# Four GpSimd instructions in halves, with new orders, PSUM homes and waits, in an attention and slot-mixture kernel

## The chip, the cores and the metric

One core of one Trainium2 chip. The metric is the device time of one execution in microseconds; the kernel before took 595.33 us (median of 3 runs, 594.32 to 596.03).

## The reference, cut to what matters

```python
x = x + layernorm(attention(layernorm(x)))          # x: 32 batches x 256 tokens x 128
x = x + layernorm(slot_mixture(layernorm(x)))

def attention(x):                                   # 16 heads of 8
    q, k, v = exp(x Wq' + bq), exp(x Wk' + bk), x Wv' + bv
    kv  = cumsum(k[:, :, :, None] * v[:, :, None, :], axis=1)   # outer products, summed over tokens
    k1  = cumsum(k, axis=1)
    out = einsum('zsD,zsDd->zsd', q, kv) / sum(q * k1)
    return out Wo' + bo

def slot_mixture(x):                                # 8 experts x 64 slots = 512 slots
    logits   = rms_norm(x) . rms_norm(slot_embeds)
    slots    = xn weighted by softmax(logits over tokens)       # "dispatch"
    hidden   = gelu(slots @ w1)                     # 512 wide
    out      = (hidden @ w2) weighted by softmax(logits over slots)  # "combine"
```

## The kernel before, in words

The kernel is written in raw instructions, one list for each engine, with a semaphore for nearly every kind of result. The unit of work is a batch of 256 tokens: partition p holds the tokens 2p and 2p+1 (the even and the odd token of a pair). There are 32 batches, and each goes through the stages below. Many batches are under way at once: in step `s` TensorE projects batch s, sums the keys of batch s-1, closes the attention of s-2, starts the slots of s-3, and does the hidden layer of s-4.

**The path of one batch n.**
- `x_statistics` (VectorE), `x_rstd_of` (GpSimd: a floor `x_ve` and a power `x_rs`), `x_normalise` (VectorE, writes `xh`), `x_transpose` (TensorE), `xT_high` (ScalarE) and `xT_low` (VectorE): the value is split into a high part and the rest, since a product is made of three matmuls (`three`, L800 to 804) to keep precision. Then `project(n, 0)` and `project(n, 1)`, and `qk_evict`, `v_evict` (ScalarE) into `E`.
- `shift_odd` (SyncE's DMA) moves the keys and values of the odd tokens one partition on, into `prev`.
- GpSimd builds the pair sums: `outer_odd` writes `kv_prev` from `prev`, `outer_even` writes `kv` from `E` (both through the helper `outer`, L211, 1024 elements a partition), `pair_sum` adds them (L380), `pair_keys` adds the keys (L374). ScalarE's `sums_high` copies them to `kv_hi` (L435), and GpSimd's `sums_low` writes the rest `kv_lo` (L318, 1152 elements). The two outer products, the pair sum and `sums_low` are GpSimd's four long instructions.
- `cumulate(n, k)` for k = 2, 0, 1 (TensorE, a triangular matrix) makes the running sums in PSUM (`CU[k]`), `multiply(n, k)` (VectorE) multiplies each with q into `prod`, `attention_sums` reduces `prod` into `ND` in PSUM. `own_product` (GpSimd), `own_sum` (VectorE), `own_value` (GpSimd) make the even token's share of its own pair; `attention` adds it and divides.
- `att_transpose`, `attT_copy`, `attention_out`, `y_squares`, `y_rstd_of` (GpSimd), `first_residual` (VectorE), `x1_squares`, `x1_rstd_of` (GpSimd: a floor, then a power), `x1_normalise` (VectorE, writes `xn`), `xn_transpose`, `xnT_high`, `xnT_low`, `logits`.
- `slot_maxima` and `part_maxima` (VectorE), `dispatch_exp` (ScalarE), `part_transpose`, `token_maxima`, `subtract_max`, `dispatch_scale` (VectorE: a reciprocal, and a multiply of `disp_t` by it, L1331), `dispatch_transpose`, `dispatch_copy`, `combine_exp`, `gather_slots`, `slT_high`, `slT_low`, `hidden(n, f)` for four f, `gelu(n, f)`, `process`, `proc_copy`, `mixture`, `o_squares`, `o_rstd_of`, `second_residual`, `store`.

**What sets the order.** Each engine has its own list: `first_steps`, then `step(s)` for all s, then `last_steps` (some engines have none). An engine does its list strictly in order. A stage waits only where its producer isn't known to be done by another wait already made; that is why many waits stand under `if n in (...)`. ScalarE changes its table between the exponentials and the GELUs twice a step (`gelu_table`, `exp_table`, L426 and L430).

**PSUM.** Eight banks are named by hand (L147 to L161). Tensors that share a bank can't be alive together; before, the running sums 1 and 2 share bank 5, so that `cumulate(n, 1)` waits until `multiply(n, 2)` has read the bank.

`spin(k)` runs k matmuls on the identity whose result nobody reads. They fill TensorE's idle time in `first_steps`.

Of the kernel before, what the change touches and what calls it, by code (L numbers as in the profile page):

```python
# [5 lines left out]
def attention_and_slot_mixture(  # L6
# [7 lines left out]
    F32 = mybir.dt.float32  # L14
# [37 lines left out]
    with ctx:  # L52
# [6 lines left out]
        def sem(name):  # L59
# [99 lines left out]
        HP = [banks[:, 6, :], banks[:, 0, :], banks[:, 6, :], banks[:, 4, :]]  # L159
        PR = banks[:, 6, :].rearrange("p (j d) -> p j d", d=DIM)  # L160
        OB = banks[:, 5, 0:NC * YW].rearrange("p (c d) -> p c d", d=YW)  # L161
# [22 lines left out]
        xT_lo_ready, qk_exp, v_copied, kv_even, kv_odd, kv_den = (  # L184
            sem("s_" + n) for n in ("xTlo", "qkexp", "vcopy", "kve", "kvo", "kvd"))
        kv_built, kv_hi_ready, kv_lo_ready, qk_own_ready, own_den, own_ready = (
            sem("s_" + n) for n in ("kv", "kvhi", "kvlo", "qkown", "ownden", "own"))
        own_added, summed, den_ready, att_ready, att_T, attT_ready = (
            sem("s_" + n) for n in ("ownadd", "summed", "deninv", "att", "attTp", "attT"))
        wo_done, y_var, y_rstd, x1_ready, x1_var, x1_floor = (  # L190
            sem("s_" + n) for n in ("wo", "yve", "yrs", "x1", "x1ve", "x1fl"))
        x1_rstd, xn_ready, xnT_done, xnT_hi_ready, xnT_lo_ready, lb_done = (
            sem("s_" + n) for n in ("x1rs", "xn", "xnT", "xnThi", "xnTlo", "lb"))
        max_ready, part_ready, partT_done, tok_ready, lb_shifted, disp_exp = (
            sem("s_" + n) for n in ("max", "part", "partT", "tok", "lbs", "dexp"))
        disp_inverted, disp_scaled, slT_done, slT_hi_ready, slT_lo_ready, proc_ready = (
            sem("s_" + n) for n in ("dinv", "dscale", "slT", "slThi", "slTlo", "procs"))
        mix_done, o_var, o_rstd, res_ready, x_stat = (
            sem("s_" + n) for n in ("mix", "ove", "ors", "res", "xstat"))
# [28 lines left out]
        def _(sp):  # L228
# [45 lines left out]
        def _(pool):  # L274
# [1194 lines left out]
```

## Time and profile before

| what | value |
|---|---|
| median of three runs | 595.33 us |
| the profiled execution: own time, span | 594.64 us, 592.9 us |
| TensorE busy, share of the span | 557.5 us, 94% |
| VectorE | 484.2 us, 82% |
| ScalarE | 473.4 us, 80% |
| GpSimd | 473.1 us, 80% |
| instructions | 10573 |

In the profile PE is TensorE's matmuls and PEld its weight loads, DVE is VectorE, ACT ScalarE, POOL GpSimd, SP SyncE. A line number is one of the kernel before. Where an arrow stands between two tiles, the left one is written from the right one. The 1.7 us between span and own time are outside the first and last instruction.

### The profile page before, as it was taken

The numbers are of one execution on the slowest core, as the hardware profiler recorded it, in microseconds if no ns is written. First come the engines' busy times: TensorE is split into PE (matmuls) and PEld (weight loads), VectorE is DVE, ScalarE is ACT, GpSimd is POOL, SyncE is SP. The second block draws the span as 40 slices with busy tenths as digits, with TensorE's granted clock in tenths as the row PEclk, the third lists the DMA queues.
The fourth block names the chain that finished last, engine by engine and source line by source line (L and its number), as shares of the span: only waits on it lengthen the run. The fifth ranks groups of instructions, "written<-read, shape, count | busy, mean of one in ns | idle before, by whom it ended". The sixth has DMA issues, their size and how long they took to land.

```text
span 592.9 us, 10573 instructions
## 1 busy us (share of the span) xinstructions
PE 557.5 (94%) x3772; PEld 486.1 (82%) x3772; DVE 484.2 (82%) x922; ACT 473.4 (80%) x1244; POOL 473.1 (80%) x462
## 2 busy tenths in 40 slices
PE   7937999999999999999999999999999999999886
PEld 7925898888888898888888988888888988887775
DVE  4897888888988888888888888889888888878430
ACT  3255889988888889888888899888888888888663
POOL 4777888889888988889888888898888888974100
PEclk9958999999999999999999999999999999999999
DMA  4000000000000000000000000000000000000000
GB/s 115 10 19 19 19 9 19 19 28 28 27 28 28 10 28 18 28 28 28 28 27 28 10 26 20 28 28 28 28 27 12 26 19 28 19 26 10 11 9 19
DMA packets 16825, 14.29 MB, mean 24 GB/s; under 512 B 2850, under 2 KB 16644, under 8 KB 16772
## 3 DMA queue, kind: packets, MB, share of 16 engines
q1 hardware_dynamic: 14708, 12.76, 7.1%
q10 hardware_dynamic: 2064, 0.86, 0.6%
q8 instruction: 30, 0.49, 0.3%
q14 instruction: 23, 0.19, 0.1%
HBM read 5.25 MB, written 4.19 MB: 16 GB/s over the span
## 4 chain that ended last, share of the span: by engine, by line
PE 42%; POOL 23%; ACT 19%; DVE 10%; issue 3%; DMA 1%; SPq 0%; POOLq 0%; DVEq 0%; ACTq 0%
POOL kv_lo L318 11%; PE banks L929 9%; PE banks L955 8%; POOL x_rs L296 7%; ACT kv_hi L422 6%; ACT L430 6%; PE banks L802 5%; PE banks L804 5%; PE banks L803 5%; DVE prod L1253 4%; ACT hid L447 3%; DVE xh L1157 3%; PE banks L782 3%; PE banks L881 2%; ACT disp_t L545 2%
## 5 line engine op out<-in xcount | busy, mean ns | idle before, releaser
L942 PE MATMUL banks<-w_c,hid 128*128 128x128 f32 x1024 | 124.6, 276 | 2.4 <-ACT hid L447 2.4
L942 PEld LDWEIGHTS banks<-w_c,hid 128*128 128x128 f32 x1024 | 119.2, 192 | 3.5 <-ACT hid L447 2.2
L318 POOL TENSOR_TENSOR kv_lo<-kv,kv_hi 128x1152 fp32r<-128x1152 f32 x31 | 81.7, 2636 | 32.5 <-ACT kv_hi L422 32.5
L1253 DVE TENSOR_TENSOR prod<-banks,E 128x768 f32<-128x768 f32 x96 | 88.3, 948 | 1.9 <-PE banks L882 1.9
L1268 DVE TENSOR_REDUCE banks<-prod 128x288 f32<-128x2304 f32 x32 | 81.5, 2545 | 0.0
L212 POOL TENSOR_TENSOR kv_prev<-prev 128x1024 f32<-128x1024 f32 x31 | 66.8, 2153 | 10.5 <-DMA prev<-E 10.5
L955 PEld LDWEIGHTS banks<-proc,comb 128*128 128x128 f32 x512 | 61.1, 191 | 17.0 <-DVE prod L1253 14.9
L380 POOL TENSOR_TENSOR kv<-kv,kv_prev 128x1024 f32<-128x1024 f32 x31 | 74.7, 2410 | 0.0
L447 ACT ACTIVATE hid<-banks 128x512 f32<-128x512 f32 x128 | 70.5, 612 | 4.8 <-PE banks L804 2.0
L212 POOL TENSOR_TENSOR kv<-E 128x1024 f32<-128x1024 f32 x32 | 68.6, 2144 | 4.1 <-ACT E L422 2.2
L1318 DVE TENSOR_REDUCE neg_max<-banks 128x4 f32<-128x1024 f32 x32 | 39.2, 1224 | 31.2 <-PE banks L804 31.2
L955 PE MATMUL banks<-proc,comb 128*128 128x129 f32 x512 | 62.5, 275 | 0.8 <-ACT proc L422 0.8
L929 PE MATMUL banks<-disp,xn 128*128 128x512 f32 x128 | 60.7, 597 | 1.1 <-ACT disp L422 1.0
L545 ACT ACTIVATE disp_t<-banks,neg_max 128x256 f32<-128x256 f32 x128 | 58.9, 474 | 0.0
L802 PE MATMUL banks<-slT_hi,w_hi 128*128 128x512 f32 x128 | 54.7, 427 | 0.2 <-DVE slT_lo L1178 0.2
L422 ACT ACTIVATE disp<-banks 128x512 f32<-128x512 f32 x64 | 34.7, 595 | 23.4 <-PE banks L910 23.4
L881 PE MATMUL banks<-kv_hi,tri 128*128 128x384 f32 x96 | 41.4, 432 | 10.7 <-DVE prod L1253 9.3
L804 PE MATMUL banks<-slT_hi,w_lo 128*128 128x512 f32 x128 | 50.7, 396 | 0.0
L803 PE MATMUL banks<-slT_lo,w_hi 128*128 128x512 f32 x128 | 50.6, 395 | 0.0
L296 POOL TENSOR_TENSOR x_rs<-x_ve,minus_half 128x2 f32<-128x2 f32 x32 | 47.9, 1495 | 2.7
L346 POOL TENSOR_TENSOR o_rs<-o_ve,minus_half 128x2 f32<-128x2 f32 x32 | 22.8, 712 | 29.1 <-ACT o_sq L482 29.1
L426 ACT ACT_TABLE_LOAD x31 | 39.8, 1283 | 0.6
(140 smaller groups left out, 1516.9 us busy)
## 6 DMA issues: line engine op xcount, KB each, us to landing
X<-in_L_attn_x_dram SPq DMA_DIRECT2D x32, 128.0 KB, 2.1
out_dram<-res SPq DMA_DIRECT2D x32, 128.0 KB, 2.0
prev<-E SPq DMA_DIRECT2D x32, 112.0 KB, 2.1
w_in<-in_L_ffn_w_dram ACTq DMA_DIRECT2D x2, 256.0 KB, 4.6
prev<-E SPq DMA_DIRECT2D x32, 15.0 KB, 2.0
se_in<-n_L_ffn_slot_embeds_dram ACTq DMA_DIRECT2D x1, 256.0 KB, 3.2
w_in<-in_L_attn_Wq_dram SPq DMA_DIRECT2D x1, 64.0 KB, 2.4
w_in<-in_L_attn_Wk_dram SPq DMA_DIRECT2D x1, 64.0 KB, 2.2
```

The costliest lines, as they stand in the source:

```text
L212: return eng.tensor_tensor(dst.rearrange("p (d h e) -> p d h e", d=HD, h=NH), k.rearrange("p (o h e) -> p o h e", o=1, h=NH).broadcast_to( ...
L296: pool.tensor_tensor(x_rs[:, :], x_ve[:, :], minus_half[:, 0:NC], ALU.pow).then_inc(x_rstd, 1)
L318: pool.tensor_tensor(kv_lo[:, :], kv[:, :], kv_hi[:, :].bitcast(F32), ALU.subtract)\
L447: act.activation(hid[:, f, :], HP[f], ACT.Gelu).then_inc(gelu_ready[f], 1)
L802: pe.matmul(dst, a_hi, b_hi, start=start, stop=False, skip_group_check=True)
L803: pe.matmul(dst, a_hi, b_lo, start=False, stop=False, skip_group_check=True)
L804: return pe.matmul(dst, a_lo, b_hi, start=False, stop=stop, skip_group_check=True)
L929: last = pe.matmul(SL, xn[n % 2][:, c, :], disp[:, c, :], start=(c == 0), stop=(c == NC - 1))
L942: last = pe.matmul(PR[:, j, :], hid[:, f, j * P:(j + 1) * P], w2_c[:, f, :], start=(f == 0), stop=(f == FJ - 1))
L955: last = pe.matmul(OB[:, c, :], comb[n % 2][:, j, c * P:(c + 1) * P], proc[:, j, 0:YW], start=(j == 0), stop=(j == SJ - 1))
L1253: dve.tensor_tensor(prod[u][:, :, d0 * DIM:d1 * DIM].rearrange("p c (d f) -> p c d f", d=g), CU[k].rearrange("p (o d f) -> p o d f", o=1, ...
L1268: dve.tensor_reduce(ND.rearrange("p c f h -> p c (f h)"), prod[n % 2][:, :, :].rearrange("p c (f e) -> p c f e", e=HD), AX.X, ALU.add).the ...
```

## The change

Four kinds of edit, made together.

1. **Halves.** `outer` gets a parameter `parts`; GpSimd's two outer products, its pair sum and its `sums_low` are two instructions of half the length each, and the semaphore is raised by the second. The first batch's outer product on VectorE stays whole.
2. **Orders.** In GpSimd's step `x_rstd_of`, `o_rstd_of` come ahead of `sums_low`, and `own_product` and `y_rstd_of` behind it; `own_value` comes ahead of `outer_even`. In VectorE's step `x_normalise` comes ahead of `dispatch_scale`, `own_sum` behind `x1_normalise`, `attention` goes to the start of the next step ahead of the maxima, and the part maxima come ahead of the slot maxima. In TensorE's step `cumulate(., 1)` comes behind the next `x_transpose`, `hidden(., 3)` ahead of `hidden(., 0)`, and `att_transpose` between the two projections. In ScalarE's step `v_evict` comes directly behind `qk_evict`.
3. **PSUM homes.** The running sum 1 has bank 1 and no longer shares with sum 2; the outputs, transposes and hidden tiles move.
4. **Waits** follow the new orders: `cumulate(n, 1)` waits for `x1_ready` of n-1 (bank 1's last reader) in place of `prod_ready`; `dispatch_exp` waits for `max_ready`; `hidden(n, 3)` waits for `slT_lo_ready`; `project(n, 1)` waits for `gelu_ready[2]`.

The first steps get more `spin` (73 in place of 8 after the first running sum), and `last_steps` fall away on VectorE and ScalarE and are written anew on GpSimd.

```diff
-        XT = banks[:, 1, 0:SEQ]
-        XN = banks[:, 3, 0:SEQ]
-        PT = banks[:, 7, 0:SEQ]
-        CU = [banks[:, 6, 0:DU * DIM], banks[:, 5, 0:DU * DIM], banks[:, 5, 0:DU * DIM]]
+        XT = banks[:, 4, 0:SEQ]
+        XN = banks[:, 6, 0:SEQ]
+        PT = banks[:, 5, 0:SEQ]
+        CU = [banks[:, 6, 0:DU * DIM], banks[:, 1, 0:DU * DIM], banks[:, 5, 0:DU * DIM]]
...
-        HP = [banks[:, 6, :], banks[:, 0, :], banks[:, 6, :], banks[:, 4, :]]
+        HP = [banks[:, 4, :], banks[:, 0, :], banks[:, 1, :], banks[:, 1, :]]
...
+        def outer(eng, dst, k, v, parts=1):
+            w = HD // parts
+            for d in range(0, HD, w):
+                last = eng.tensor_tensor(
+                    dst[:, d * DIM:(d + w) * DIM].rearrange("p (d h e) -> p d h e", d=w, h=NH),
+                    k.rearrange("p (o h e) -> p o h e", o=1, h=NH).broadcast_to((P, w, NH, HD)),
+                    v.rearrange("p (h d o) -> p d h o", d=HD, o=1)[:, d:d + w].broadcast_to((P, w, NH, HD)), ALU.mult)
+            return last
...
             def sums_low(n):
                 pool.wait_ge(kv_hi_ready, n + 1)
-                pool.tensor_tensor(kv_lo[:, :], kv[:, :], kv_hi[:, :].bitcast(F32), ALU.subtract)\
+                for f in (slice(0, FEAT // 2), slice(FEAT // 2, FEAT)):
+                    last = pool.tensor_tensor(kv_lo[:, f], kv[:, f], kv_hi[:, f].bitcast(F32), ALU.subtract)
+                last\
                     .then_inc(kv_lo_ready, 1)
...
             def pair_sum(n):
                 pool.wait_ge(kv_even, n + 1)
-                pool.tensor_tensor(kv[:, 0:KVF], kv[:, 0:KVF], kv_prev[:, :], ALU.add).then_inc(kv_built, 1)
+                for f in (slice(0, KVF // 2), slice(KVF // 2, KVF)):
+                    last = pool.tensor_tensor(kv[:, f], kv[:, f], kv_prev[:, f], ALU.add)
+                last.then_inc(kv_built, 1)
...
             def step(s):                      # GpSimd
                 x_rstd_of(s)
+                o_rstd_of(s - 6)
+                sums_low(s - 2)
+                x_negative(s - 2)
+                own_product(s - 2)
                 y_rstd_of(s - 3)
                 outer_odd(s - 1)
                 x1_rstd_of(s - 3)
                 pair_keys(s - 1)
-                x_negative(s - 2)
+                own_value(s - 2)
                 outer_even(s - 1)
-                own_value(s - 2)
                 pair_sum(s - 1)
-                o_rstd_of(s - 5)
-                own_product(s - 1)
-                sums_low(s - 1)
...
             def step(s):                      # VectorE
                 x_statistics(s)
+                attention(s - 3)
+                part_maxima(s - 4)
+                slot_maxima(s - 4)
                 second_residual(s - 6)
                 token_maxima(s - 4)
-                own_sum(s - 2)
+                x_normalise(s)
                 dispatch_scale(s - 4)
-                x_normalise(s)
                 multiply(s - 2, 2)
                 first_residual(s - 3)
                 multiply(s - 2, 0)
                 multiply(s - 2, 1)
                 xT_low(s)
                 x1_normalise(s - 3)
+                own_sum(s - 2)
                 slT_low(s - 4)
                 attention_sums(s - 2)
                 xnT_low(s - 3)
-                attention(s - 2)
-                slot_maxima(s - 3)
-                part_maxima(s - 3)
...
             def step(s):                      # TensorE
                 x_transpose(s)
+                cumulate(s - 2, 1)
                 gather_slots(s - 4)
                 mixture(s - 5)
                 xn_transpose(s - 3)
+                hidden(s - 4, 3)
                 hidden(s - 4, 0)
-                hidden(s - 4, 3)
                 hidden(s - 4, 1)
                 hidden(s - 4, 2)
                 logits(s - 3)
                 project(s, 0)
+                att_transpose(s - 2)
                 project(s, 1)
-                att_transpose(s - 2)
...
                 cumulate(s - 1, 0)
-                cumulate(s - 1, 1)
...
             def step(s):                      # ScalarE
                 exp_table(s)
                 sums_high(s - 2)
                 qk_evict(s - 1)
+                v_evict(s - 1)
                 attT_copy(s - 3)
                 dispatch_exp(s - 4)
-                v_evict(s - 1)
...
                 xT_high(s)
+                combine_exp(s - 4, 1)
                 slT_high(s - 4)
-                combine_exp(s - 4, 1)
                 gelu_table(s - 4)
                 xnT_high(s - 3)
+                gelu(s - 4, 3)
                 o_squares(s - 5)
                 gelu(s - 4, 0)
-                gelu(s - 4, 3)
...
             def cumulate(n, k):
...
                 elif k == 1:
-                    pe.wait_ge(prod_ready[2], n + 1)
+                    if n == 0:
+                        after(pe, v_copied, n + 1)
+                    after(pe, x1_ready, n - 1)
...
             def dispatch_exp(n):
-                act.wait_ge(part_ready, n + 1)
-                if n == 30:
-                    act.wait_ge(max_ready, n + 1)
+                act.wait_ge(max_ready, n + 1)
```

## Rows read from the trace of the kernel before

**Rows 1.** The page: busy time and share of the span.

```profile
PE 557.5 (94%) x3772; PEld 486.1 (82%) x3772; DVE 484.2 (82%) x922; ACT 473.4 (80%) x1244; POOL 473.1 (80%) x462
```

**Rows 2.** Timeline, ScalarE: `sums_high` of batches 2 and 31 (start, duration).

```profile
48.12 1.16 ACT L422 ACTIVATE kv_hi<-kv 128x1152 fp32r<-128x1152 f32 x1
...
533.85 1.16 ACT L422 ACTIVATE kv_hi<-kv 128x1152 fp32r<-128x1152 f32 x1 [0.68 <-POOL kv L380]
```

**Rows 3.** The chain of waits in one step (start, length in us, what).

```profile
300.66 2.63 POOL kv_lo L318
...
303.65 1.66 POOL x_rs L296
...
305.33 0.60 DVE xh L1157 x2
```

**Rows 4.** Windows: stretch, length; busy (count) PE, PEld, DVE, ACT, POOL; clock, DMA, GB/s.

```profile
97.99:114.32 16.33, 16.33 (x115) 14.52 (x114) 14.62 (x29) 14.41 (x39) 14.61 (x15) 1.00 0.09 26
299.42:316.20 16.78, 16.49 (x115) 14.45 (x114) 14.65 (x29) 14.57 (x38) 15.00 (x15) 1.00 0.08 25
```

**Rows 5.** The waits, whole span: total, times, longest in us.

```profile
PEld banks L881 <- DVE prod L1253: 18.5, 29, 2.2
```

**Rows 6.** Timeline, VectorE and GpSimd where their instructions overlap.

```profile
303.51 1.23 DVE L1331 TENSOR_TENSOR disp_t<-disp_t,disp_inv 128x1024 f32<-128x1024 f32 x1
...
102.22 0.70 POOL L296 TENSOR_TENSOR x_rs<-x_ve,minus_half 128x2 f32<-128x2 f32 x1
102.89 1.16 POOL L334 TENSOR_TENSOR y_rs<-y_ve,minus_half 128x2 f32<-128x2 f32 x1
...
102.25 1.24 DVE L1331 TENSOR_TENSOR disp_t<-disp_t,disp_inv 128x1024 f32<-128x1024 f32 x1
...
19.90 2.55 POOL L212 TENSOR_TENSOR kv_prev<-prev 128x1024 f32<-128x1024 f32 x1 [0.79 <-DMA prev<-E]
...
20.38 2.15 DVE L1157 TENSOR_SCALAR xh<-X,x_mv,x_rs 128x128 f32<-128x128 f32 x1
...
309.48 0.46 POOL L374 TENSOR_TENSOR kv<-E,prev 128x128 f32<-128x128 f32 x1
309.55 0.48 DVE L1299 TENSOR_SCALAR xn<-x,x_mv,x_rs 128x128 f32<-128x128 f32 x1
```

**Rows 7.** Groups of GpSimd's instructions, 200 to 400 us: count, busy, mean ns, idle.

```profile
L318 POOL TENSOR_TENSOR kv_lo<-kv,kv_hi 128x1152 fp32r<-128x1152 f32 x12 | 31.6, 2637 | 12.3 <-ACT kv_hi L422 12.3
L380 POOL TENSOR_TENSOR kv<-kv,kv_prev 128x1024 f32<-128x1024 f32 x12 | 29.0, 2417 | 0.0
...
L326 POOL TENSOR_TENSOR own<-E,own 128x128 f32<-128x128 f32 x12 | 6.7, 558 | 0.0
```

**Rows 8.** Timeline of GpSimd, VectorE and TensorE in the step of rows 3.

```profile
306.26 2.15 POOL L212 TENSOR_TENSOR kv_prev<-prev 128x1024 f32<-128x1024 f32 x1 [0.29 <-DMA prev<-E]
...
308.80 0.71 POOL L341 TENSOR_TENSOR x_rs<-x_vf,minus_half 128x2 f32<-128x2 f32 x1
...
302.72 0.28 DVE L1262 TENSOR_REDUCE own<-qk_own 128x16 f32<-128x128 f32 x1
...
310.21 0.68 DVE L1178 TENSOR_TENSOR slT_lo<-banks,slT_hi 128x512 fp32r<-128x512 f32 x1
...
311.14 0.19 PEld L802 LDWEIGHTS banks<-slT_hi,w_hi 128*128 128x128 f32 x1
...
317.44 2.64 POOL L318 TENSOR_TENSOR kv_lo<-kv,kv_hi 128x1152 fp32r<-128x1152 f32 x1 [1.06 <-ACT kv_hi L422]
```

**Rows 9.** The first steps: a window's row, and the chain's row on the spins.

```profile
35.00:40.00 5.00, 3.28 (x12) 2.67 (x12) 4.13 (x11) 1.51 (x8) 3.93 (x5) 0.50 0.08 28
...
15.07 8.93 PE banks L782 x80
```

**Rows 10.** Timeline, the last batch: VectorE's slot maxima and ScalarE's table load.

```profile
566.76 1.22 DVE L1318 TENSOR_REDUCE neg_max<-banks 128x4 f32<-128x1024 f32 x1 [2.00 <-PE banks L804]
...
568.07 1.28 ACT L545 ACT_TABLE_LOAD   x1
```

More of the change, by code:

```diff
@@ L190, in attention_and_slot_mixture @@
[L190 to L197, printed above, removed]
@@ new lines, in attention_and_slot_mixture @@
+        y_var, y_rstd, x1_ready, x1_var, x1_floor, x1_rstd = (
+            sem("s_" + n) for n in ("yve", "yrs", "x1", "x1ve", "x1fl", "x1rs"))
+        xn_ready, xnT_done, xnT_hi_ready, xnT_lo_ready, lb_done, max_ready = (
+            sem("s_" + n) for n in ("xn", "xnT", "xnThi", "xnTlo", "lb", "max"))
+        part_ready, partT_done, tok_ready, lb_shifted, disp_exp, disp_inverted = (
+            sem("s_" + n) for n in ("part", "partT", "tok", "lbs", "dexp", "dinv"))
+        disp_scaled, slT_done, slT_hi_ready, slT_lo_ready, proc_ready, mix_done = (
+            sem("s_" + n) for n in ("dscale", "slT", "slThi", "slTlo", "procs", "mix"))
@@ L201, in after @@
+        o_var, o_rstd, res_ready, x_stat = (
+            sem("s_" + n) for n in ("ove", "ors", "res", "xstat"))
         def after(eng, s, n):
@@ L406, in step, with last_steps @@
                 pair_keys(s - 1)
-                x_negative(s - 2)
+                own_value(s - 2)
                 outer_even(s - 1)
-                own_value(s - 2)
                 pair_sum(s - 1)
-                o_rstd_of(s - 5)
-                own_product(s - 1)
-                sums_low(s - 1)
+            def last_steps():
+                x_rstd_of(31)
+                o_rstd_of(25)
+                sums_low(29)
+                x_negative(29)
+                own_product(29)
+                y_rstd_of(28)
+                outer_odd(30)
+                pair_keys(30)
+                x1_rstd_of(28)
+                own_value(29)
+                outer_even(30)
+                pair_sum(30)
+                o_rstd_of(26)
+                sums_low(30)
+                x_negative(30)
+                own_product(30)
+                y_rstd_of(29)
+                outer_odd(31)
+                x1_rstd_of(29)
+                pair_keys(31)
+                own_value(30)
+                outer_even(31)
+                pair_sum(31)
+                o_rstd_of(27)
+                sums_low(31)
+                x_negative(31)
+                own_product(31)
+                y_rstd_of(30)
+                x1_rstd_of(30)
+                own_value(31)
+                o_rstd_of(28)
+                y_rstd_of(31)
+                x1_rstd_of(31)
+                o_rstd_of(29)
+                o_rstd_of(30)
+                o_rstd_of(31)
             first_steps()
-            for s in range(3, 37):
+            for s in range(5, 31):
                 step(s)
+            last_steps()
         @block.scalar
@@ L773, in _ @@
             first_steps()
-            for s in range(8, 33):
+            for s in range(6, 37):
                 step(s)
-            last_steps()
         @block.tensor
@@ L1128, in _ @@
             first_steps()
-            for s in range(6, 32):
+            for s in range(6, 34):
                 step(s)
```

421 lines of the change are left out of this document (125 added, 296 removed).

## The prediction

> **What bounds the kernel now.** I read the page's busy times first [rows 1]: TensorE leads with 94%, but three others lie at 80 to 82%, and an average doesn't say which wait ends last. So next the pace of the steps. ScalarE's `sums_high` stands at 48.12 us for batch 2 and at 533.85 for batch 31 [rows 2]: 485.73 us for 29 steps, 16.75 each; 48 us lie ahead of it and 59 behind. Then the chain of waits inside one step [rows 3]. It doesn't stay on TensorE: it goes `kv_lo` 2.63 and `x_rs` 1.66 on GpSimd, `xh` 0.60 and `prod` on VectorE, and by the running sum 1, gather, mixture and hidden matmuls on TensorE back to ScalarE and `kv_hi`. That ring is one step long.
>
> The windows of two steps show what the ring costs [rows 4]. Both hold 115 matmuls. The usual one is 16.78 us long, the rare one 16.33, and in the rare one TensorE is busy for all of it: 16.33 is TensorE's own length of a step, the floor. The 0.45 between them is where `cumulate(n, 1)` waits for `multiply(n, 2)` to empty bank 5, 18.5 us in 29 waits over the span [rows 5].
>
> The timeline says why `x_rs` takes 1.66 [rows 6]. `disp_t` (VectorE, both inputs in SBUF) runs from 303.51 to 304.74; `x_rs` starts at 303.65 [rows 3] and ends at 305.31, 0.57 after it. In the rare step `x_rs` started 0.03 ahead of `disp_t` and took 0.70, and the next one, `y_rs`, took 1.16 and ended 0.56 after `disp_t`. So a small GpSimd instruction that comes second stands until `disp_t` is over. The other way round, `xh` started at 20.38 under a long GpSimd instruction (19.90 to 22.45) and took 2.15, to 22.53, 0.08 after it. Behind a short one (0.46, from 309.48) `xn` took 0.48 where one of a free pair takes some 0.34 (0.60 for two [rows 3]): 0.14 lost, so the short one gives way 0.21 after its start.
>
> **The change part by part.**
>
> *Bank 1 for sum 1, moved behind the next transpose.* The wait of rows 5 goes. `cumulate(n, 1)` now waits for `x1_ready` of n-1, a pair of 0.3 us instructions done before `multiply(n, 0)`, and has the transpose as slack. If this were all that binds, a step would take TensorE's 16.33: 29 x (16.75 - 16.33) = 12.2 us gained.
>
> *`x_rstd` ahead of `sums_low`.* It leaves the ring of rows 3 with 2.63 + 1.66: it is done while ScalarE still writes `kv_hi`, and `x_normalise` no longer waits for it. What is late next is the rest of GpSimd's list.
>
> *The halves.* What does one more instruction cost? The pair sum takes 2.42 for 1024 elements [rows 7], the pair keys 0.46 for 128 [rows 6]: 2.19 ns an element, 0.18 fixed. The outer product, 2.15 for 1024 [rows 8]: (2.15 - 0.46) / 896 = 1.89 ns, 0.22 fixed. Instructions in a row overlap by 0.03 [rows 6]. So a split adds 0.14 to the pair sum, 0.19 to each outer product, and 0.14 to `sums_low`, 0.66 a step. Nearest rows for bounds: 0 (the fixed part wholly hidden in the first half) and 0.46 each, a whole 128-element instruction. I take 0.66, since both shapes give it. The gain of halves is that a VectorE instruction held by GpSimd waits for half.
>
> *Who holds whom in the new order.* Let e be the end of `sums_low`. Take the step's first hidden matmul, 311.14, as zero: `sums_low` starts at 6.3 (317.44), and its first half ends at 7.7. `x_normalise` now comes behind `token_maxima`, where `own_sum` stood before: 302.72 + 16.78 = 319.50, at 8.4 [rows 8]. So `xh` arrives in the second half and stands until e: first of the pair done at e+0.08, second 0.26 later, reciprocal 0.2, and `disp_t` may start at e+0.47. GpSimd does `x_negative` and then starts `own_product` at about e+0.45 (an estimate from its 0.19 us, its 0.07 gaps and `xh` in between). It is first by a hair; as with `xn`, it gives way 0.21 after its start. `disp_t` runs e+0.68 to e+1.91. `y_rstd` waits for it: e+2.47 (the 0.56 above). Then the ring through GpSimd goes on:
> - `outer_odd` 2.15 + 0.19 less the overlap: e+4.77 [rows 8]. Its DMA is early, since `v_evict` moved ahead of the exponentials.
> - `x1_rstd`: 306.26 + 2.15 = 308.41 to 308.80 + 0.71 = 309.51 [rows 8], 1.10: e+5.87.
> - `xn` pair behind the pair keys, 309.55 to 310.21 [rows 6, 8], 0.66, and 0.04 to wake: e+6.57. `own_sum` 0.28 [rows 8] and 0.05: e+6.90. `own_value`, now ahead of `outer_even`, waits for it (the pair keys cover 0.46 of this 1.03): 0.56 [rows 7], e+7.42.
> - `outer_even` 2.15 + 0.19: e+9.76. `pair_sum` is directly behind, so its wait costs 0.07, then 2.42 + 0.14: e+12.39.
> - `x_rstd` free of `disp_t` 1.01, `o_rstd` 0.66: e+14.06. `sums_low` 2.64 + 0.14 less overlap 0.02: e+16.82.
>
> So the ring through GpSimd alone is 16.82 us, 0.49 above TensorE's floor. A second ring goes by `slT_low`: 0.68 from e+6.85 and 0.05, then 6.3 from the first hidden matmul to `sums_low` (311.14 to 317.44), and 2.76: 6.85 + 0.73 + 6.3 + 2.76 = 16.64 [rows 8]. It is shorter and hidden. The first one decides: 29 x (16.82 - 16.75) = +2.0 us. The released bank is worth nothing then: TensorE waits elsewhere, 0.49 a step ahead of the dispatch transposes and the hidden matmuls.
>
> *A rule weighed.* In the rows only a VectorE instruction with one SBUF tensor is held by GpSimd; `disp_t` never comes second. The Trainium skill, "SBUF — State Buffer", section "Who interferes with whom", says that a VectorE instruction with two SBUF inputs and a GpSimd one that reads SBUF exclude each other whichever is first. By it `own_product` holds `disp_t` as in the sum; without it `disp_t` ends 0.21 earlier and the ring is 16.61. Rows 6 agree with one direction (`x_rs` held 0.93), no row shows the other.
>
> *First steps.* Until 24 us all goes as before (39 spins in place of 40; a spin is 8.93 / 40 = 0.22 us [rows 9]). Behind it 73 spins come in place of 8, 14.5 us more, in idle time of TensorE of about that length. They keep the clock up: it was 0.50 between 35 and 40 us [rows 9]. `logits(0)` is on the chain at half speed and gets back some 1.4 us, but `w1_low`, `wo_centre` now stand ahead of `bo_centre` on VectorE, and `pair_sum(2)` ends some 1 us later. I take -0.5 (bounds -3, full clock and the halves' shorter stand; +3, spins that overrun a wait).
>
> *The end.* For batch 31 ScalarE's exponentials waited for the slot maxima, done at 567.98, while the table load started at 568.07 behind a GELU [rows 10]. Now the part maxima come first, 1.14 (566.76 to 567.90, where they stood second): +1.1 on the path to the end. Bounds 0 and +3 for the rest of the redone tail.
>
> *Edits at nothing.* `hidden(., 3)` first, `att_transpose` between the projections and `combine_exp` ahead of `slT_high` move equal work along queues with slack of 0.2 or more; if that is gone, TensorE waits up to 0.2 a step, still under its 0.49 of spare time. `attention` in the next step fills VectorE's wait for the logits (about 1 us). `v_evict` ahead of `attT_copy` puts 0.3 before a transpose that has it.
>
> Sum: 594.64 + 2.0 - 0.5 + 1.1 = 597.2 us against the profiled execution; that one lies 0.7 under the median of the three runs, so 597.5 is as good. I say 597.3.
>
> **The rivals.**
>
> *TensorE takes over (faster).* If halves in a row hide their fixed part (0.66 off: 16.16), or `xh` slips in between the halves of `sums_low` so that `disp_t` starts by e, the GpSimd ring falls under 16.33 and TensorE decides. 29 x 0.42 = 12.2 off: 594.64 - 12.2 + 0.6 = 583; with half of the split cost hidden, 16.49, 588. For it: TensorE's 16.33 has been seen [rows 4]. Against it: both fixed costs read the same from two shapes.
>
> *`disp_t` first, `own_product` held (slower).* The race at e+0.45 against e+0.47 can go the other way. Then `disp_t` ends at e+1.70, `own_product` 0.32 behind it and `y_rs` 0.70 later, at e+2.74 in place of 2.47. The ring is 17.09: 29 x 0.34 = 9.9 over, 605. It decides from the point where `x_negative` loses 0.02 more. For it: `x_rs` lost just such a race in nearly every step.
>
> *VectorE's pair of SBUF inputs isn't held by GpSimd.* Ring 16.61, 29 x 0.14 = 4.1 off, 591.
>
> **How the numbers follow.** Chances: the forecast 0.45, its own range 592 to 601 by 0.15 a step either way; TensorE's floor 0.25; `disp_t` first 0.20; not held 0.10. Within 0.3% is 593.5 to 597.1, about what can be told from no change. The forecast lies at its upper edge, so of its 0.45 I give 0.10 to faster, 0.15 to the same, 0.20 to slower. Faster: 0.10 + 0.25 + 0.08 = 0.43. Same: 0.15 + 0.02 = 0.17. Slower: 0.20 + 0.20 = 0.40. The range 584 to 604.5 leaves out the lowest of TensorE's case and the upper edge of the race.
>
> **What would show it.** The wait of `cumulate(., 1)` on `prod` is gone. `x_rs` takes 0.70 and `y_rs` more than 1, ending 0.56 behind `disp_t`. One of the `xh` pair takes over 0.7. Halves of about 1.18 and 1.3. GpSimd is over 90% busy with next to no idle before `kv_lo`, steps of 16.8. Steps of 16.3 with TensorE always busy, or `own_product` at 1.4 us, would prove a rival. It is wrong at its root if neither engine shows longer instructions where the two overlap.

## The result, and the profile after

The changed kernel takes 592.36 us against 595.2 for the one before, each the median of 20 executions side by side: a ratio of 0.9948, 95% interval 0.9933 to 0.9963. It is 0.5% faster. The prediction was 597.3 us, 0.3% slower: the range held the time, and the sign was wrong. The interval lies clear of no change.

The page after: busy times, and the shares of the chain that ended last.

```profile
PE 567.5 (96%) x3908; PEld 501.8 (85%) x3908; DVE 509.7 (86%) x922; ACT 470.7 (80%) x1244; POOL 493.5 (84%) x587
...
POOL 74%; DVE 8%; PE 7%; issue 5%; ACT 4%; DMA 1%; SPq 0%; POOLq 0%; DVEq 0%
```

TensorE still leads in the first line, as in [rows 1], but the chain lies on GpSimd for 74% of the span. That TensorE is the busiest engine says nothing here of which one sets the pace. Next `kv_hi` of batches 2 and 31 (timeline, ScalarE), to set beside [rows 2].

```profile
47.69 1.16 ACT L484 ACTIVATE kv_hi<-kv 128x1152 fp32r<-128x1152 f32 x1 [2.27 <-POOL kv L382]
...
532.56 1.16 ACT L484 ACTIVATE kv_hi<-kv 128x1152 fp32r<-128x1152 f32 x1 [1.05 <-POOL kv L382]
```

With the spans (592.9 before, 590.2 after) these rows cut the difference in three, the cuts of the prediction's own sum:

| stretch | before | after | difference | predicted |
|---|---|---|---|---|
| to `kv_hi` of batch 2 | 48.12 | 47.69 | -0.43 | -0.5 |
| 29 steps | 485.73 | 484.87 | -0.86 | +2.0 |
| behind `kv_hi` of batch 31 | 59.05 | 57.64 | -1.41 | +1.1 |

The chain of waits through one step after (start, length, what; against [rows 3]), from the start of one `kv_lo` to the next:

```profile
299.45 2.75 POOL kv_lo L319 x2
...
302.54 0.45 POOL qk_own L352
303.00 1.64 POOL y_rs L335
304.63 2.26 POOL kv_prev L213 x2
...
308.03 0.73 DVE xn L1216 x2
...
309.04 0.52 POOL own L327
309.56 2.26 POOL kv L213 x2
...
311.88 2.54 POOL kv L382 x2
...
314.78 0.71 POOL x_rs L296
315.49 0.67 POOL o_rs L347
316.16 1.39 POOL kv_lo L319
```

It is the ring that the prediction drew, piece by piece: all of it on GpSimd, but for `xn` and `own_sum`, and 16.71 long from 299.45 to 316.16. In this step it never goes to TensorE. (A length in the chain leaves out what overlaps with the piece before; the timeline's lengths of the same instructions are up to 0.04 longer.) What holds `y_rs` at 1.64 is seen in the timeline of VectorE and GpSimd (e, the end of `sums_low`, is 302.20):

```profile
301.12 1.44 DVE L1075 TENSOR_SCALAR xh<-X,x_mv,x_rs 128x128 f32<-128x128 f32 x2
...
302.54 0.45 POOL L352 TENSOR_TENSOR qk_own<-E 128x128 f32<-128x128 f32 x1
302.67 1.40 DVE L1246 TENSOR_TENSOR disp_t<-disp_t,disp_inv 128x1024 f32<-128x1024 f32 x1
302.95 1.68 POOL L335 TENSOR_TENSOR y_rs<-y_ve,minus_half 128x2 f32<-128x2 f32 x1
```

`xh` takes 1.44 for the pair where it took 0.60 in [rows 3], and ends at 302.56, behind e. `disp_t` starts 0.13 behind `own_product` (tile `qk_own`) and takes 1.40 where it took 1.23 in [rows 6]. `y_rs` ends 0.56 behind `disp_t`.

TensorE's waits after, whole span. The row of [rows 5] has none that answers to it; this one stands in its place (0.44 a step on the weight loads):

```profile
PEld banks L863 <- DVE disp_t L1246: 13.6, 31, 0.9
```

### The profile page after: what moved, and what is told of

Read it like the earlier page. It is cut to its first block, busy times and chain, and to the rows that moved or that the text cites. A ratio compares the mean times of both kernels' runs of the same rounds, so it can differ in the third digit from the quotient of the medians.

```text
span 590.2 us, 10874 instructions
## 1 busy us (share of the span) xinstructions
PE 567.5 (96%) x3908; PEld 501.8 (85%) x3908; DVE 509.7 (86%) x922; ACT 470.7 (80%) x1244; POOL 493.5 (84%) x587
## 4 chain that ended last, share of the span: by engine, by line
POOL 74%; DVE 8%; PE 7%; issue 5%; ACT 4%; DMA 1%; SPq 0%; POOLq 0%; DVEq 0%
POOL kv_lo L319 13%; POOL kv L382 12%; POOL kv_prev L213 11%; POOL kv L213 11%; POOL y_rs L335 8%; DVE xn L1216 4%; POOL x_rs L342 4%; POOL x_rs L296 3%; POOL o_rs L347 3%; POOL own L327 3%; POOL qk_own L352 2%; PE banks L743 2%; POOL x_vf L340 1%; DVE own L1179 1%; ACT disp_t L602 1%
## 5 line engine op out<-in xcount | busy, mean ns | idle before, releaser
L319 POOL TENSOR_TENSOR kv_lo<-kv,kv_hi 128x576 fp32r<-128x576 f32 x62 | 86.0, 1409 | 2.1 <-ACT kv_hi L484 2.1
L511 ACT ACTIVATE hid<-banks 128x512 f32<-128x512 f32 x128 | 73.5, 606 | 13.1 <-PE banks L764 12.7
L382 POOL TENSOR_TENSOR kv<-kv,kv_prev 128x512 f32<-128x512 f32 x62 | 78.8, 1292 | 2.4
L213 POOL TENSOR_TENSOR kv<-E 128x512 f32<-128x512 f32 x64 | 73.3, 1167 | 2.1 <-ACT E L484 2.1
L213 POOL TENSOR_TENSOR kv_prev<-prev 128x512 f32<-128x512 f32 x62 | 70.8, 1160 | 0.2 <-DMA prev<-E 0.2
L883 PE MATMUL banks<-disp,xn 128*128 128x512 f32 x128 | 63.0, 614 | 1.5 <-ACT disp L484 1.5
L335 POOL TENSOR_TENSOR y_rs<-y_ve,minus_half 128x2 f32<-128x2 f32 x32 | 52.0, 1624 | 10.8 <-ACT y_sq L529 10.8
L1228 DVE TENSOR_REDUCE part_max<-banks 128x256 f32<-128x1024 f32 x32 | 39.2, 1225 | 9.0 <-PE banks L764 6.4
L1246 DVE TENSOR_TENSOR disp_t<-disp_t,disp_inv 128x1024 f32<-128x1024 f32 x32 | 44.3, 1384 | 1.1
L1075 DVE TENSOR_SCALAR xh<-X,x_mv,x_rs 128x128 f32<-128x128 f32 x64 | 41.6, 690 | 1.1 <-POOL x_rs L296 1.1
```

The lines of the kernel that those rows point to most:

```text
L213: last = eng.tensor_tensor(dst[:, d * DIM:(d + w) * DIM].rearrange("p (d h e) -> p d h e", d=w, h=NH), k.rearrange("p (o h e) -> p o h e", ...
L319: last = pool.tensor_tensor(kv_lo[:, f], kv[:, f], kv_hi[:, f].bitcast(F32), ALU.subtract)
L335: pool.tensor_tensor(y_rs[:, :], y_ve[:, :], minus_half[:, 0:NC], ALU.pow).then_inc(y_rstd, 1)
L382: last = pool.tensor_tensor(kv[:, f], kv[:, f], kv_prev[:, f], ALU.add)
L511: act.activation(hid[:, f, :], HP[f], ACT.Gelu).then_inc(gelu_ready[f], 1)
L883: last = pe.matmul(SL, xn[n % 2][:, c, :], disp[:, c, :], start=(c == 0), stop=(c == NC - 1))
```

## The experiments

Names: "after" is the changed kernel. Every time is the median of a kernel's executions, and every ratio is against the kernel before, executed on the same chip in the same round of runs; its medians there were 595.3 to 595.7.

### 1. What each group of edits is worth alone

**All four long instructions whole again**, the rest as after (`a_whole`):

```diff
-                for f in (slice(0, FEAT // 2), slice(FEAT // 2, FEAT)):     # sums_low
+                for f in (slice(0, FEAT),):
-                outer(pool, kv[:, 0:KVF], ..., 2)                           # outer_even, outer_odd too
+                outer(pool, kv[:, 0:KVF], ...)
-                for f in (slice(0, KVF // 2), slice(KVF // 2, KVF)):        # pair_sum
+                for f in (slice(0, KVF),):
```

> The changed kernel with its four long GpSimd instructions whole again, all else kept. Theory 1 (the ring through GpSimd is 16.70 us a step and a split costs 0.11 or 0.12 on it, four times): the ring falls by 0.45 to 16.25, TensorE's 16.33 takes over, steps of 16.33 to 16.40, total 9 to 11 us less than the changed kernel (about 582), idle time before kv_lo comes back. Theory 2 (the halves are what gained, since VectorE stands for half as long): xh and disp_t stand longer, steps of 16.8 or more, total 3 us or more above the changed kernel.

Measured: 581.95 us, ratio 0.9776 (0.9753 to 0.9798). A window of 200 us (busy times of PE, PEld, DVE, ACT, POOL; after, PE has 197.51 there), and behind it one `kv_lo` in the timeline:

```profile
200.00:400.00 200.00, 200.00 (x1379) 177.68 (x1378) 187.84 (x342) 176.44 (x464) 183.50 (x171) 1.00 0.09 25
```

```profile
294.33 2.64 POOL L319 TENSOR_TENSOR kv_lo<-kv,kv_hi 128x1152 fp32r<-128x1152 f32 x1 [0.20 <-ACT kv_hi L484]
```

TensorE is busy for all of it, steps are 16.38, and GpSimd waits 0.20 for `kv_hi` in each. The halves cost 10.4 us here. The other edits together are worth 13.3 (595.2 to 581.95). How they share it between orders, PSUM homes and spins is not shown by these two kernels.

**The other way round: the kernel before with the four halves and nothing else** (`b_halves`; the same edits as in the change's diff).

> The kernel before with the four instructions in halves and nothing else. Theory 1: its ring holds one split, that of sums_low, 0.11 a step; the other three (0.35) fit in the 1.05 us idle before kv_lo. Steps of 16.89, total 3.2 us more than before (1.005). Theory 2 (halves gain by themselves): the same or less than before.

Measured: 604.11 us, ratio 1.0144 (1.0122 to 1.0166), steps of 17.06. Slower as expected, but by 8.6 in place of 3.2. Timeline, GpSimd and the `disp_t` of the same step:

```profile
306.10 2.78 POOL L322 TENSOR_TENSOR kv_lo<-kv,kv_hi 128x576 fp32r<-128x576 f32 x2 [0.84 <-ACT kv_hi L428]
308.97 1.26 POOL L297 TENSOR_SCALAR x_ve<-x_mv 128x2 f32<-128x2 f32 x1
310.31 0.70 POOL L299 TENSOR_TENSOR x_rs<-x_ve,minus_half 128x2 f32<-128x2 f32 x1
...
308.95 1.22 DVE L1337 TENSOR_TENSOR disp_t<-disp_t,disp_inv 128x1024 f32<-128x1024 f32 x1
```

The split of `sums_low` pushed `x_ve` 0.02 behind the start of `disp_t`, so both `x_ve` and, after it, `x_rs` come late: from the end of `kv_lo` to the end of `x_rs` it is 2.13 here and 2.02 in the kernel before ([rows 3]: 303.29 to 305.31). With the split itself (2.78 for 2.64) that makes 0.25 of the 0.28 a step.

### 2. What a split costs, and where

Two kernels with some halves only. **Only `sums_low` in halves** (`a_half_low`), and **only the two outer products** (`a_half_outer`):

```diff
 # a_half_low: outer_even, outer_odd, pair_sum as in a_whole; sums_low keeps
                 for f in (slice(0, FEAT // 2), slice(FEAT // 2, FEAT)):
 # a_half_outer: sums_low, pair_sum as in a_whole; both outer products keep
                 outer(pool, ..., 2)
```

> The kernel after with three of the four long GpSimd instructions whole again; only sums_low stays in two halves. Theory 1 (a split adds 0.11 to 0.12 us to GpSimd's list, and the step is the longer of GpSimd's ring and TensorE's 16.38): with all four whole GpSimd has 0.20 us of idle time ahead of kv_lo in a step of 16.38, so its list is 16.18; one split makes it 16.29, still under 16.38. Steps of 16.38, idle time ahead of kv_lo about 0.09, total 582, the same as with all four whole. Theory 2 (every split costs its share, a quarter of the 10.4 us between the kernel after and the one with four whole): 16.46 a step, 584.6.

> The kernel after with sums_low and the pair sum whole again; only the two outer products stay in halves. Theory 1: GpSimd's list is 16.18 + 2 x 0.115 = 16.41, 0.03 over TensorE's 16.38: steps of 16.41 to 16.45, total 583 to 584, no idle time of GpSimd ahead of kv_lo, each outer product 2.26 in two. Theory 2 (every split costs a quarter of the 10.4 us): 16.54 a step, 587.

Measured: 586.64 us (ratio 0.9842, 0.9816 to 0.9868) with steps of 16.52, and 584.47 us (0.9808, 0.9783 to 0.9832) with steps of 16.44. The second has theory 1's steps, and lies 0.5 above its time. The first fell outside both theories. Its rows, a wait of TensorE over the span and one `kv_lo`:

```profile
PEld banks L863 <- DVE disp_t L1246: 9.4, 31, 0.9
```

```profile
296.62 2.77 POOL L319 TENSOR_TENSOR kv_lo<-kv,kv_hi 128x576 fp32r<-128x576 f32 x2 [0.19 <-ACT kv_hi L484]
```

GpSimd still idles 0.19 ahead of `kv_lo`, so its list isn't the bound, and yet a step is 0.14 longer. The weight loads of the dispatch transposes (L863) wait for `disp_t` in 31 batches; in `a_whole` the same row has only 4. So there is a second ring (not the prediction's, which went by `slT_low`): through `sums_low`, `xh`, `disp_t`, the dispatch transposes and the TensorE work behind them to `kv_hi`. `sums_low` lies in both rings, the other three only in GpSimd's. The split of `sums_low` costs its full 0.14 a step; the two of the outer products cost 0.06 together, since in `a_whole` GpSimd's list had 0.2 of idle time for them.

What a split costs must be read like for like. The timeline's lengths of the four pairs of halves, after:

```profile
299.42 2.78 POOL L319 TENSOR_TENSOR kv_lo<-kv,kv_hi 128x576 fp32r<-128x576 f32 x2
...
304.60 2.29 POOL L213 TENSOR_TENSOR kv_prev<-prev 128x512 f32<-128x512 f32 x2
...
309.51 2.29 POOL L213 TENSOR_TENSOR kv<-E 128x512 f32<-128x512 f32 x2
311.88 2.54 POOL L382 TENSOR_TENSOR kv<-kv,kv_prev 128x512 f32<-128x512 f32 x2
```

The same of `a_whole`, beside its `kv_lo` of 2.64 above:

```profile
290.00 2.40 POOL L382 TENSOR_TENSOR kv<-kv,kv_prev 128x1024 f32<-128x1024 f32 x1
...
299.37 2.14 POOL L213 TENSOR_TENSOR kv_prev<-prev 128x1024 f32<-128x1024 f32 x1
...
304.13 2.15 POOL L213 TENSOR_TENSOR kv<-E 128x1024 f32<-128x1024 f32 x1
```

`sums_low` 0.14 more, the outer products 0.15 and 0.14, the pair sum 0.14: a split costs GpSimd 0.14, whichever of the four it is, 0.56 a step for all. The steps say the same. GpSimd's list in `a_whole` is 16.38 less 0.20 of idle time and the 0.03 that it would overlap without it, 16.15; with two splits it is 16.44 (`a_half_outer`), with four 16.71. The 0.11 and 0.12 of the expectations came from setting the chain's lengths of the halves (2.75, 2.26) against the timeline's of the whole ones.

### 3. The new bank

**`cumulate(n, 1)` waits for `multiply(n, 2)` again**, in after (`a_prodwait`) and in `a_whole` (`a_whole_prodwait`), where TensorE is the bound and a late bank would show:

```diff
                     after(pe, x1_ready, n - 1)
+                    pe.wait_ge(prod_ready[2], n + 1)
```

> The changed kernel in which cumulate(n, 1) waits again for multiply(n, 2), as if it still shared its bank; its place behind the transpose is kept. Theory 1 (the bank's release is worth nothing as long as GpSimd's ring is longer than TensorE's step): TensorE waits 0.1 to 0.5 a step for prod, and the total stays within 0.5 us of the changed kernel, at 592. Theory 2 (the release is what gained): 5 to 12 us more.

> The kernel after with all four long instructions whole, where cumulate(n, 1) also waits for multiply(n, 2), as it had to while it shared a bank with the running sum 2. Here TensorE is the bound (busy for the whole of a step), so a late bank would be seen. Theory 1: multiply(n, 2) ends at 316.09 and cumulate(n, 1) starts after the transposes at some 316.8, 0.7 later: the wait is over when it comes, steps stay at 16.38, total 582 within 0.5; the new bank is worth nothing, and the old wait of 0.6 came from a late xh ahead of multiply(n, 2). Theory 2 (the new bank is what lets TensorE run without a gap): steps of 16.6 or more, 588 and above.

Measured: 592.98 us (0.9951, 0.9931 to 0.9971) against after's 592.36, and 582.62 us (0.9773, 0.9749 to 0.9798) against 581.95, with steps of 16.71 and 16.38. The 0.62 and 0.67 more are a little over the 0.5 allowed, but in the profiled executions the first running sum, ahead of the edit's first place, is already 0.67 and 0.60 later (24.02 to 24.69, 24.11 to 24.71), so that isn't the edit's. The 0.1 to 0.5 a step that TensorE was to wait for `prod` didn't come: in both kernels it waits for it once, 0.6 us in the first steps. In its new place the wait costs nothing that can be measured. What let TensorE off the 18.5 us of [rows 5] are the orders. The edit puts back the wait alone: sum 1 keeps bank 1, and `cumulate(n, 1)` its wait for `x1_ready`, which came with it. What the bank would have been worth in the old place wasn't tried.

### 4. The orders

**`own_product` ahead of `sums_low`**, in after (`a_own_first`) and in `a_whole` (`a_whole_own_first`):

```diff
+                own_product(s - 2)
                 sums_low(s - 2)
                 x_negative(s - 2)
-                own_product(s - 2)
```

> The changed kernel with own_product moved ahead of sums_low in GpSimd's step, halves kept. Theory 1 (what stands between the end of sums_low and outer_odd is priced by who holds whom): nothing holds disp_t (1.23 in place of 1.40), y_rs starts ahead of it and takes 0.70 in place of 1.68, the first half of outer_odd stands until disp_t is over. The ring loses about 0.9 there and gets 0.45 in front of sums_low: 16.25 to 16.35, total 9 to 11 us less than the changed kernel. Theory 2 (only GpSimd's sum of work counts, an order is worth nothing): steps of 16.7 and no difference.

> The kernel after with all four long instructions whole and own_product ahead of sums_low. GpSimd's 0.20 of idle time ahead of sums_low takes 0.20 of own_product's 0.45, so sums_low starts 0.25 later in both rings; disp_t is not held (1.23 in place of 1.41), y_rs takes 0.70. Theory 1 (TensorE's ring by sums_low and disp_t decides): 16.38 + 0.25 - 0.18 = 16.45 a step, 584. Theory 2 (GpSimd's list decides, and it gets shorter by 1.0): TensorE's 16.38 stays the bound, 582.

Measured: 592.64 us (0.9955, 0.9936 to 0.9973), where 9 to 11 less were expected, and 582.35 us (0.9775, 0.9750 to 0.9799), theory 2's. Timeline of `a_own_first`:

```profile
300.59 0.46 POOL L352 TENSOR_TENSOR qk_own<-E 128x128 f32<-128x128 f32 x1
301.00 2.78 POOL L319 TENSOR_TENSOR kv_lo<-kv,kv_hi 128x576 fp32r<-128x576 f32 x2
...
302.51 1.63 DVE L1075 TENSOR_SCALAR xh<-X,x_mv,x_rs 128x128 f32<-128x128 f32 x2
...
304.12 0.70 POOL L335 TENSOR_TENSOR y_rs<-y_ve,minus_half 128x2 f32<-128x2 f32 x1
304.25 1.22 DVE L1246 TENSOR_TENSOR disp_t<-disp_t,disp_inv 128x1024 f32<-128x1024 f32 x1
...
306.22 1.09 ACT L484 ACTIVATE disp<-banks 128x512 f32<-128x512 f32 x2 [1.10 <-PE banks L863]
...
308.15 0.23 POOL L340 TENSOR_SCALAR x_vf<-x_v 128x2 f32<-128x2 f32 x1 [0.53 <-ACT x_sq L537]
```

`disp_t` and `y_rs` came as expected in `a_own_first`, 1.22 and 0.70, and the time didn't move. With e = 303.78, the end of `sums_low`, `x_vf` starts at e+4.37, where it was e+4.77 after: of the 0.9 only 0.40 is gained, since GpSimd now waits 0.53 for ScalarE's `x_sq`. That stands behind the dispatch copies (tile `disp`) in ScalarE's list, these wait for the dispatch transposes, and these for `disp_t` (TensorE waits for it 14.8 us in 30 waits); `xh` ahead of `disp_t` is held to e. And `own_product` puts 0.41 ahead of `sums_low`, from 300.59 to 301.00. 0.40 less and 0.41 more: the step is 16.73. This isn't the second ring of `a_half_low`, since GpSimd doesn't wait for `kv_hi` here: it is GpSimd's own list from `x_vf` to e, closed by `xh`, `disp_t`, the transposes, the copies and `x_sq`. So the number is theory 2's, the reason isn't.

In `a_whole_own_first` `disp_t` takes 1.22, but `y_rs`, late by a wait of 0.29 for ScalarE, starts 0.10 behind it and takes 1.68, not 0.70. TensorE's 16.38 is the bound with or without this edit.

**`x_rstd` back behind `sums_low`**, in `a_whole` (`a_whole_xr_back`):

```diff
-                x_rstd_of(s)
                 o_rstd_of(s - 6)
                 sums_low(s - 2)
+                x_rstd_of(s)
```

> The kernel after with all four long instructions whole and x_rstd back behind sums_low, as before the change. Theory 1 (in the new order xh is made between sums_low and disp_t, and TensorE's ring runs by sums_low, xh, disp_t and the dispatch transposes; it is 16.38 long with disp_t starting 0.47 behind the end e of sums_low): x_rs now ends at e + 1.0, the xh pair takes 0.6, disp_t starts at e + 1.85, 1.4 later; its own stand of 0.18 goes. Steps of 17.6 to 17.8, total 612 to 622, with TensorE waiting for disp_t over 1 us a step. Theory 2 (GpSimd has the same work in either order, and only its sum counts): 16.4 a step, 582.

Measured: 619.38 us, ratio 1.0401 (1.0375 to 1.0428), steps of 17.78, and 43.4 us of the wait for `disp_t`: theory 1. Given the rest of the new order, this one move is worth 37.4 us. It can't be read as its worth in the kernel before, which had `disp_t` ahead of `xh`.

**`disp_t` ahead of `xh`**, as before, in `a_whole` (`a_whole_disp_first`):

```diff
-                x_normalise(s)
                 dispatch_scale(s - 4)
+                x_normalise(s)
```

> The kernel after with all four long instructions whole and disp_t's multiply ahead of xh on VectorE, as before the change. token_maxima ends at 296.31 in the step where sums_low runs from 294.33 to 296.97, so disp_t starts at about 296.5, second, under a long GpSimd instruction. Theory 1 (GpSimd's instruction holds it): disp_t takes 1.23 + 0.47 = 1.7 us, to 298.2; x_negative stands behind it, own_product comes at 298.7 and y_rs ends near 299.9 in place of 299.40: GpSimd's list 16.18 + 0.5 = 16.7 a step, total near 590. Theory 2 (disp_t is not held by a GpSimd instruction that came first): disp_t takes 1.23, ends at 297.7, and the total is 582 to 585.

Measured: 593.18 us, ratio 0.9959 (0.9944 to 0.9975), steps of 16.79, the pace of the kernel before. The size lay near theory 1's, its mechanism didn't occur:

```profile
302.96 0.18 DVE L1244 RECIPROCAL disp_inv<-disp_sum 128x4 f32<-128x4 f32 x1 [0.83 <-ACT disp_t L602]
303.12 0.46 POOL L352 TENSOR_TENSOR qk_own<-E 128x128 f32<-128x128 f32 x1
303.18 1.49 DVE L1246 TENSOR_TENSOR disp_t<-disp_t,disp_inv 128x1024 f32<-128x1024 f32 x1
...
305.97 0.59 DVE L1208 SCALAR_TENSOR_TENSOR x<-banks,y_rs,X 128x128 f32<-128x128 f32 x2
```

```profile
PEld banks L839 <- DVE x L1208: 13.7, 31, 0.5
```

`disp_t` waited for ScalarE's exponentials until `sums_low` was over (302.79), and `xh`, `multiply(n, 2)` and `first_residual` (tile `x`) stood behind it. The second fence is TensorE's wait in this kernel, in every step: the running sum 1 (L839) waits for `first_residual`, the last reader of its new bank 1. So here the wait that came with the new PSUM home does bind. In `a_whole` `xh` fills VectorE's wait for the exponentials, and `first_residual` comes in time (0.6 us in 3 waits). Whether a long GpSimd instruction holds `disp_t` for its whole length stays open; the two rows with the short one give 1.40 and 1.49.

The other moves of the change (`hidden(., 3)`, `att_transpose`, `own_value`, `v_evict`, `attention`) weren't tried one by one.

### 5. The two ends

**8 spins in place of 73** behind the first running sum, in `a_whole` (`a_whole_few_spins`):

```diff
-                spin(27)
+                spin(3)
...
-                spin(7)      # and 1, 4, 7, 12, 12, 3 left out
+                spin(5)
```

> The kernel after with all four long instructions whole and, behind the first running sum, 8 spin matmuls as before the change in place of 73. Theory 1 (the spins keep TensorE's clock up in the first steps): the granted clock between 30 and 45 us is 0.50 to 0.67 in place of 1.00, and kv_hi of batch 2 starts 1 to 2 us later than 47.3; the total 583 to 584. Theory 2 (the first steps are bound by VectorE and GpSimd, and TensorE's clock does not show in the time): clock down as well, kv_hi of batch 2 within 0.3 of 47.3, total 582.

Measured: 583.70 us (0.9796, 0.9771 to 0.9822) against 581.95. The clock fell, to 0.73 over 30 to 45 us where 0.50 to 0.67 was expected, from 1.00 in `a_whole` (TensorE was busy 6.59 us of the 15 there, in place of 14.55). `kv_hi` of batch 3, in `a_whole` and then with few spins:

```profile
63.76 1.17 ACT L484 ACTIVATE kv_hi<-kv 128x1152 fp32r<-128x1152 f32 x1
```

```profile
65.91 1.17 ACT L484 ACTIVATE kv_hi<-kv 128x1152 fp32r<-128x1152 f32 x1
```

It is 2.15 later. 0.85 of that is there already at `kv_hi` of batch 1 (29.51 and 30.36), and the first running sum, ahead of any spin left out, is as late (24.11 and 25.00). So it isn't the spins' doing: that mark lies anywhere from 29.15 to 30.65 in the kernels here. The other 1.30 come between batches 2 and 3, one batch later than expected, and up to batch 2 the pace is the same (17.80). There `logits(0)` takes 2.73 (45.86 to 48.59, clock 0.50 over 45 to 50 us) in place of 1.53 (44.96 to 46.49, clock 1.00). So the spins are worth 1.3 us by this one pair of profiled executions; the medians differ by 1.75.

**A single wait for batch 30** in the kernel before (`b_one_wait`):

```diff
-                act.wait_ge(part_ready, n + 1)
                 if n == 30:
                     act.wait_ge(max_ready, n + 1)
+                else:
+                    act.wait_ge(part_ready, n + 1)
```

> The kernel before, where the exponentials of batch 30 wait for the slot maxima alone in place of both maxima's semaphores; nothing else differs. Theory 1 (a table load goes ahead of a single wait, and stays behind the first of two): the table load of batch 30 starts behind the last GELU ahead of it, near 549 to 551 in place of 552.61, and the exponentials start 1.2 to 1.3 us earlier; about 1.2 us less in all, in the stretch behind kv_hi of batch 31. Theory 2 (the load's place has nothing to do with the waits): table load still at 552.6, no change.

Measured: 594.17 us (0.9967, 0.9950 to 0.9984). Timeline, the kernel before and then this one:

```profile
550.18 1.23 DVE L1312 TENSOR_REDUCE part_max<-banks 128x256 f32<-128x1024 f32 x1 [1.05 <-PE banks L804]
...
551.32 1.21 DVE L1318 TENSOR_REDUCE neg_max<-banks 128x4 f32<-128x1024 f32 x1
552.61 1.28 ACT L545 ACT_TABLE_LOAD   x1 [1.34 <-DVE neg_max L1318]
```

```profile
550.68 1.23 DVE L1313 TENSOR_REDUCE part_max<-banks 128x256 f32<-128x1024 f32 x1 [1.05 <-PE banks L805]
...
551.78 1.28 ACT L546 ACT_TABLE_LOAD   x1
```

From the start of `part_max` to the table load it is 2.43 before and 1.10 here: with one wait the load goes ahead of it, 0.02 behind the GELU. With two it starts 0.08 behind the end of `neg_max`, so behind both waits, and not only the first as the expectation has it. From `kv_hi` of batch 31 to the span's end it is 592.1 - 534.33 = 57.77, 1.28 less than before. Theory 1 holds for the time.

## Why the prediction was wrong

**What held.** The ring through GpSimd: all its pieces, in order, and its place as the bound. `own_product` first, `disp_t` held, `y_rs` 0.56 behind it; the released bank worth nothing in this order; `x_rs` at 0.71 and the wait of [rows 5] gone; the first steps -0.43 for -0.5, and the clock at 1.00 where it was 0.50 [rows 9]. By the rule of the Trainium skill, "SBUF — State Buffer", section "Who interferes with whom", a GpSimd instruction that comes first holds a VectorE one with two SBUF inputs; the trace agrees, with 1.40 against 1.23, and 1.22 again with `own_product` out of the way.

**The first step that failed: "So a split adds 0.14 to the pair sum, 0.19 to each outer product, and 0.14 to `sums_low`".** It is 0.14 for all four: right for the pair sum and `sums_low`, 0.05 too much for each outer product. The fixed part was read from a line between the long instruction and a 128-element one, the pair keys. That one is a plain sum of rows, as the pair sum is, and there the line was good; the outer product reads broadcast rows, and the line gave 0.22 fixed for it. That the form is the reason was not tested. The 0.10 too much a step is 2.9 us over 29 steps, all that lies between +2.0 and -0.86. The ring by the prediction's own marks, from the end e of one `sums_low` to the next:

| piece | predicted | after |
|---|---|---|
| to the end of `y_rs` | 2.47 | 2.43 |
| `outer_odd` | 2.30 | 2.26 |
| `x1_rstd` | 1.10 | 1.11 |
| `xn`, `own_sum`, `own_value` | 1.55 | 1.56 |
| `outer_even` | 2.34 | 2.25 |
| `pair_sum` | 2.63 | 2.61 |
| `x_rstd`, `o_rstd` | 1.67 | 1.74 |
| `sums_low` | 2.76 | 2.75 |
| ring | 16.82 | 16.71 |

The two outer products miss by 0.13 (0.10 of it the splits, the rest what overlaps), `pair_sum`, `sums_low` and the piece to `y_rs` by 0.07 together, and the other three give 0.09 back. Only 0.11 in 16.82, but against the old mean of 16.75 it decides the sign (the 29 steps average 16.72). The forecast was a small difference of two large numbers, inside its own bound of 0.15 a step either way.

**The second: "Now the part maxima come first, 1.14 [...]: +1.1 on the path to the end."** Its premise was misread, and a gain was overlooked. Batch 31's exponentials didn't wait for the slot maxima before: they waited for `part_ready`, and the part maxima came second:

```profile
567.90 1.22 DVE L1312 TENSOR_REDUCE part_max<-banks 128x256 f32<-128x1024 f32 x1
```

After, they wait for `max_ready`, and the slot maxima come second. Either way they wait for both. Timeline of the last batch after, to set beside [rows 10]:

```profile
564.09 1.22 DVE L1228 TENSOR_REDUCE part_max<-banks 128x256 f32<-128x1024 f32 x1 [2.69 <-PE banks L764]
564.78 0.60 ACT L511 ACTIVATE hid<-banks 128x512 f32<-128x512 f32 x1 [1.44 <-PE banks L764]
565.23 1.21 DVE L1233 TENSOR_REDUCE neg_max<-banks 128x4 f32<-128x1024 f32 x1
565.39 1.28 ACT L602 ACT_TABLE_LOAD   x1
...
566.69 0.47 ACT L602 ACTIVATE disp_t<-banks,neg_max 128x256 f32<-128x256 f32 x1
```

What comes last is the table load, which isn't held by the wait: it starts behind the GELU (565.38), and `neg_max` ends at 566.44, ahead of the load's end (before: `part_max` at 569.12, the load at 569.35). From the first maximum to the exponentials it is 2.60, as before (566.76 to 569.36). The prediction had read it itself from [rows 10], a load at 568.07 "behind a GELU", and didn't draw the consequence. So 0 in place of +1.1. The term that was missing: batch 30 lost its second wait (before, `if n == 30`): from `part_max` to the exponentials 3.73 (550.18 to 553.91) became 2.39 (548.85 to 551.24), 1.34 gained, which `b_one_wait` gives back alone as 1.28. 0 - 1.34 is nearly all of the -1.41.

Both misses point the same way: 2.9 + 2.5 = 5.4, less 0.1 in the first steps, is the 5.3 between the +2.6 of the forecast's sum and the -2.7 of the spans.

**What the prediction didn't ask** is what the orders would bring without the halves: 16.38 a step, 0.05 above the floor that it gave as TensorE's [rows 4]. Its rival "TensorE takes over" (GpSimd's ring without the splits' 0.66 at 16.16, 583 us) describes the kernel `a_whole`: GpSimd's list 16.15, 581.95 us, which beats both kernels by 2.2 and 1.8%. The halves shorten no stand on the path: `xh` is held to the end of `sums_low`, whole or in halves. In `a_whole` the pair takes 1.09 and ends 0.35 behind e, after 1.44 and 0.36; and it starts in the second half (301.12, where the first half is over at 300.84).

## What to carry to other kernels

Before cutting a long GpSimd instruction in parts so that VectorE can slip in, look whether GpSimd's own list is near the bound: each cut adds 0.14 us to it here, and in this kernel VectorE didn't slip in. Look for every ring near the bound and note which instructions lie in more than one: a change there costs at once (`sums_low`), while one that shortens a piece of one ring may only uncover the next wait (`own_product`, where `x_sq` came late). Take both lengths of a comparison from the same kind of view. And when a wait is moved or doubled, look where the table load in front of the waiting activation goes.

## What the runs showed of the hardware

- A multiply on VectorE with both inputs in SBUF (1.23 alone) that starts 0.13 or 0.06 behind a GpSimd instruction of 0.46 took 1.40 and 1.49, and ended 1.08 and 1.09 behind that one's end, 0.15 and 0.14 sooner than a start at that end would give.
- A tiny GpSimd instruction that starts 0.02 behind that multiply stands for its whole length, also one that reads a single tensor: `x_ve` (128x2) took 1.26 in place of 0.19.
- ScalarE's table load went ahead of a single wait, and stayed behind both of two: 1.33 apart from the start of `part_max`.
- An elementwise GpSimd instruction of 1024 or 1152 elements a partition took 0.14 longer in two halves, whether a sum, a difference or a product of broadcast rows.
- TensorE's busy time hides waits: `a_half_low` has it busy 199.62 of 200 us, with steps 0.14 longer than `a_whole`'s at 200.00. The pace of the steps tells.
